# Gated cross-attention block: the last batches' low parts on VectorE, a relu block moved ahead of the gates, and two swaps in the first steps

## What is computed

```python
emb = ln(x) + ctx
q, k, v = emb @ wq + bq, emb @ wk + bk, emb @ wv + bv
ek, ew = exp(k - max_k), exp(pos_bias * band - max_w)      # band: |i - j| < 64
attn = (sigmoid(q) * (ew @ (ek * v)) / (ew @ ek)) @ wo + bo
a = ln(attn + emb) * gamma + beta
ff = relu(a @ w1 + b1) @ w2 + b2                            # 256 -> 1024 -> 256
x1 = x + tanh(g_xattn) * (ln(ff + a) * gamma + beta)
n = ln(x1); prev = n shifted by one row (zeros first)
xr, xk = mu_r * n + (1 - mu_r) * prev, mu_k * n + (1 - mu_k) * prev
r = sigmoid(xr @ W_r.T); kk = relu(xk @ W_k.T) ** 2
out = x1 + tanh(g_ffn) * r * (kk @ W_v.T)
```

## Time and profile before

| | us |
|---|---|
| median of 3 runs | 482.67 |
| lowest, highest | 480.25, 482.8 |
| the profiled execution, whole | 481.42 |
| its span in the trace | 479.7 |
| PE busy in the span | 456.3 (95%) |
| PE weight loads busy | 414.6 (86%) |
| DVE, ACT, POOL busy | 392.5, 239.8, 265.8 |

### The profile page before, as it was taken

One profiled execution on the slowest core, in us unless ns is written; L12 is line 12 of the kernel. 1 busy time (PEld: TensorE's weight loads), 2 busy tenths in 40 slices (PEclk: granted clock), 3 DMA queues, 4 the chain that ended last, 5 costly groups with the idle time before them and its releaser, 6 DMA issues.

```text
span 479.7 us, 8228 instructions
## 1 busy us (share of the span) xinstructions
PE 456.3 (95%) x3080; PEld 414.6 (86%) x3080; DVE 392.5 (82%) x729; ACT 239.8 (50%) x372; POOL 265.8 (55%) x243
## 2 busy tenths in 40 slices
PE   8989989899999999999999999999999998999966
PEld 8879789789889998989889998989889996978865
DVE  4998869997959987798959988698939975788886
ACT  3681662664373634755374644655263634546242
POOL 2574852663497256853497346952495237553552
PEclk9999999999999999999999999999999999999979
DMA  8741310110002200112002200111001100020002
GB/s 267 262 131 43 113 45 2 44 56 35 0 1 89 88 2 1 44 55 79 0 1 90 87 3 1 44 45 45 0 2 42 47 2 0 1 70 20 1 0 88
DMA packets 21896, 23.35 MB, mean 49 GB/s; under 512 B 993, under 2 KB 20961, under 8 KB 21857
## 3 DMA queue, kind: packets, MB, share of 16 engines
q1 hardware_dynamic: 20768, 21.26, 13.4%
q10 hardware_dynamic: 1088, 1.57, 1.0%
HBM read 18.64 MB, written 4.19 MB: 48 GB/s over the span
## 4 chain that ended last, share of the span: by engine, by line
PE 51%; issue 16%; POOL 14%; DVE 14%; ACT 4%; DMA 1%; POOLq 0%; DVEq 0%; ACTq 0%
PE ps L1344 46%; DVE y L673 5%; POOL hid_lo L225 3%; POOL xk_lo L225 3%; PE ps L1350 2%; DVE xk L741 2%; POOL a_rows L428 2%; PE ps L1359 1%; DVE y L670 1%; POOL x_beta L428 1%; POOL emb L428 1%; DMA x_in<-in_x 1%; ACT xk_hi L1127 1%; POOL rs_head L421 1%; ACT x_in L1055 1%
## 5 line engine op out<-in xcount | busy, mean ns | idle before, releaser
L1344 PE MATMUL ps<-w_hi,hid_hi 128*128 128x256 f32 x296 | 74.6, 289 | 2.4 <-DVE y L680 1.7
L1344 PE MATMUL ps<-w_lo,hid_hi 128*128 128x256 f32 x296 | 72.9, 282 | 0.0
L817 DVE SCALAR_TENSOR_TENSOR hid_lo<-ps,neg_b,hid 128x512 fp32r<-128x512 f32 x60 | 41.2, 737 | 34.0 <-ACT hid L1175 34.0
L1344 PEld LDWEIGHTS ps<-w_hi,hid_hi 128*128 128x128 f32 x296 | 56.2, 190 | 5.4 <-DVE y L680 4.2
L1344 PEld LDWEIGHTS ps<-w_lo,hid_hi 128*128 128x128 f32 x296 | 56.1, 190 | 0.0
L673 DVE RECIPROCAL y<-y 128x512 f32<-128x512 f32 x16 | 53.6, 3353 | 0.6
L1344 PE MATMUL ps<-a_hi,w_hi 128*128 128x512 f32 x128 | 50.9, 397 | 1.0 <-ACT a_hi L1157 0.8
L1344 PE MATMUL ps<-a_hi,w_lo 128*128 128x512 f32 x128 | 50.7, 396 | 0.0
L1169 ACT ACTIVATE hid_hi<-ps,b 128x512 fp32r<-128x512 f32 x60 | 37.9, 685 | 23.0 <-PE ps L1344 23.0
L225 POOL TENSOR_TENSOR ev_lo<-res,ev_hi 128x1024 fp32r<-128x1024 f32 x8 | 19.1, 2385 | 50.1 <-ACT ev_hi L1115 50.1
L1344 PE MATMUL ps<-w_hi,hid_lo 128*128 128x256 f32 x296 | 42.8, 285 | 2.5 <-POOL hid_lo L225 1.2
(11 more groups left out here) (251 smaller groups left out, 1329.4 us busy)
## 6 DMA issues: line engine op xcount, KB each, us to landing
x_in<-in_x SPq DMA_DIRECT2D x8, 512.0 KB, 4.1
emb<-in_ctx SPq DMA_DIRECT2D x8, 512.0 KB, 3.5
x_beta<-in_x SPq DMA_DIRECT2D x8, 512.0 KB, 3.7
out<-out_sb SPq DMA_DIRECT2D x7, 512.0 KB, 2.9
hid<-in_w SPq DMA_DIRECT2D x2, 512.0 KB, 6.9
x<-in_pos ACTq DMA_DIRECT2D x1, 512.0 KB, 4.6
out_sb<-in_pos ACTq DMA_DIRECT2D x1, 512.0 KB, 6.2
x<-in_w SPq DMA_DIRECT2D x1, 512.0 KB, 4.0
```

Source lines behind the costliest of these rows:

```text
L817: dve.scalar_tensor_tensor(out=tile(lo, b, T), in0=bank(relu_pair(n, q), b), scalar=neg_b1[:, m:m + 1], in1=tile(shifted, b, T), op0=ALU.m ...
L1344: return pe.matmul(o, s, m, start=start, stop=stop, skip_group_check=True)
```

## The change

- **Tail, DVE and POOL.** `sq_low(6)`, both `last_xr_low` and the square of batch 7's first half go from POOL to DVE. POOL keeps the low part of the first half's square. `xr_low(6)` on POOL now also waits for `x1_done`, which `last_finish(0)` gives.
- **Tail, orders.** DVE: `mix_r(6)` ahead of `last_sum(0)`, `last_finish(1)` ahead of `square(6)`, `last_normalise(1)` ahead of `last_mix_k(0)`, and the new instructions in between. ACT: `relu_k(6)` ahead of `last_normalise(0)`, `last_normalise(1)` ahead of `last_xk_high(0)`, and the last tanhs and squares in another order. PE: `turn_fin(6)` behind the first of the eight `add_last`.
- **Step 7.** `hidden(6, 2)` goes ahead of `ffn_r(5)` and writes pair 1; `hidden(6, 3)` writes pair 0. `ffn_v(5)`, which follows it into pair 0, waits for 28 blocks read instead of 27. The high and low part of `xr` of batch 5 go to `ew_hi`, `ew_lo`. The turning of batch 7 goes ahead of `add_hidden(6, 3)`.
- **Start and step 1.** PE: `hidden(0, 1)` ahead of the rest of `values(1)`. DVE: `hidden_low(0, 0)` ahead of `keep_values(1)`. ACT in step 1: the normalisation of batch 3's input behind `hidden_high(0, 3)`.

```diff
         def xr_split(n):
-            return (ew_hi, ew_lo) if isinstance(n, int) and n == BATCH - 2 else (xr_hi, xr_lo)
+            return (ew_hi, ew_lo) if isinstance(n, int) and n in (BATCH - 3, BATCH - 2) else (xr_hi, xr_lo)
...
         def relu_pair(n, q):
-            return (0, 2, 1, 0)[q] if is_last(n) else (0, 2, 0, 1)[q]
+            if is_last(n):
+                return (0, 2, 1, 0)[q]
+            return (0, 2, 1, 0)[q] if isinstance(n, int) and n == BATCH - 2 else (0, 2, 0, 1)[q]
...
             last_stats("ff", 0)
+            pool.wait_ge(x1_done, TT * b + 2)
             xr_low(pool, a)
...
             last_stats("fin", 1)
-            sq_low(pool, a)
-            last_xr_low(0)
-            pool.wait_ge(relu_k_done, BATCH)
-            pool.tensor_tensor(half(last_xk_t, 0), half(last_xk_t, 0), half(last_xk_t, 0), ALU.mult).then_inc(sq_done, 1)
-            last_xr_low(1)
             pool.wait_ge(sq_hi_done, BATCH)
...
+            hidden_low(0, 0)
             keep_values(1, 3)
-            hidden_low(0, 0)
...
+            mix_r(a)
             last_sum(0)
             last_ff_stats(0)
             last_scale(0)
-            mix_r(a)
...
             last_normalise(0)
+            last_finish(1)
             square(a)
-            last_finish(1)
             last_fin_stats(1)
             last_difference(0)
+            last_normalise(1)
             last_mix_k(0)
-            last_normalise(1)
+            sq_low(dve, a)
             last_xk_low(0)
             last_mix_r(0)
             last_difference(1)
             last_mix_k(1)
+            last_xr_low(0)
+            last_xk_low(1)
             last_mix_r(1)
-            last_xk_low(1)
+            last_square(0)
+            last_xr_low(1)
             gate_ffn(a)
-            dve.wait_ge(relu_k_done, BATCH + 1)
-            dve.tensor_tensor(half(last_xk_t, 1), half(last_xk_t, 1), bank(1, 1), ALU.mult).then_inc(last_sq, 1)
+            last_square(1)
             make_out(a)
...
-                if has(e):
+                if has(e) and i > 1:
                     normalise("head", e, x_in)
                 hidden_high(b, 3)
+                if i == 1:
+                    normalise("head", e, x_in)
...
-                relus_read(most(NQ * (n + 1) + 3, NQ * BATCH))
+                relus_read(NQ * (n + 2) if n >= BATCH - 3 else NQ * (n + 1) + 3)
                 rows_out(0, unit(7, 0), sq_hi, sq_lo, sq_lo_done, n + 1, fv_done, before_low=before_low)
...
                 hidden(0, 0, 0)
+                hidden(0, 1)
 
             values(1, 3, first_hidden)
-            hidden(0, 1)
...
+                if is_last(i):
+                    pe.wait_ge(den_read, DC * BATCH)
+                    hidden(b, 2)
                 if has(a):
                     ffn_r(a)
                     pe.wait_ge(sq_done, a + 1)
-                pe.wait_ge(emb_lo_done, most(b + 3, BATCH))
-                hidden(b, 2)
+                if not is_last(i):
+                    pe.wait_ge(emb_lo_done, b + 3)
+                    hidden(b, 2)
...
                 add_hidden(b, 2)
-                add_hidden(b, 3)
+                if not is_last(i):
+                    add_hidden(b, 3)
                 pe.wait_ge(norm_done["mid"], TT * (i + 1))
                 turn(2, norm, mid_turned)
+                if is_last(i):
+                    add_hidden(b, 3)
...
-            turn_fin(a)
             pe.wait_ge(ff_sum_done, DC * b)
             for h in range(2):
                 for q in range(NQ):
                     add_last(q, h)
+                    if h == 0 and q == 0:
+                        turn_fin(a)
```

More of the change, by code:

```diff
@@ L200, in flamingo_gated_block @@
         gated_done, out_done = sem("gated_done"), sem("out_done")
-        last_norm_dve, last_sq, last_sq_lo = sem("last_norm_dve"), sem("last_sq"), sem("last_sq_lo")
+        last_norm_dve, last_sq_lo = sem("last_norm_dve"), sem("last_sq_lo")
         def after(eng, s, count):
@@ L545, in last_stats @@
                                        ).then_inc(nmr_done["fin"], 1)
[L547 to L550, removed]
             a, b = BATCH - 2, BATCH - 1
@@ L1002, in last_xk_low, with last_xr_low, last_square @@
                                   ).then_inc(xk_lo_done, 1)
+            def last_xr_low(h):
+                dve.wait_ge(xr_hi_done, BATCH + h)
+                dve.tensor_tensor(half(xr_lo, h), half(last_xr_t, h), f32(half(xr_hi, h)), ALU.subtract
+                                  ).then_inc(xr_lo_done, 1)
+            def last_square(h):
+                dve.wait_ge(relu_k_done, BATCH + h)
+                dve.tensor_tensor(half(last_xk_t, h), half(last_xk_t, h), bank(1, h), ALU.mult).then_inc(sq_done, 1)
             def last_gate(h):
@@ L1130, in mixed_r_high @@
                 act.wait_ge(xr_done, DC * (n + 1))
-                if isinstance(n, int) and n == BATCH - 2:
+                if isinstance(n, int) and n in (BATCH - 3, BATCH - 2):
                     act.wait_ge(num_done, DC * BATCH)
+                    act.wait_ge(fr_done, BATCH - 3 if n == BATCH - 3 else BATCH - 2)
                 act.activation(xr_split(n)[0], xr, ACT.Copy).then_inc(xr_hi_done, 1)
@@ L1308, in last_square_high @@
                 act.wait_ge(fv_done, b)
-                act.wait_ge(*((sq_done, BATCH) if h == 0 else (last_sq, 1)))
+                act.wait_ge(sq_done, BATCH + h)
                 act.activation(half(sq_hi, h), half(last_xk_t, h), ACT.Copy).then_inc(sq_hi_done, 1)
@@ L1321, in _ @@
             mixed_r_high(a)
+            relu_k(a)
             last_normalise(0)
-            relu_k(a)
             square_high(a)
@@ L1332, in _ @@
             last_xk_high(1)
-            last_square_high(0)
             last_tanh_r(0)
             last_xr_high(1)
+            last_square_high(0)
             last_relu_k(1)
+            last_tanh_r(1)
             last_square_high(1)
-            last_tanh_r(1)
         @block.tensor
```

## The result

The changed kernel takes 484.1 us (median of 15 runs, 480.41 to 485.58), the kernel before in the same session 480.94 (15 runs, 479.97 to 482.8). The ratio is **1.006, with a 95% interval of 1.0042 to 1.0079**: slower by 0.6%. That is just over the 0.5% that the chances took as the line, and the interval holds the line too. The prediction was 485.0, and its range of 479.5 to 488.0 holds the time. The profiled execution of the changed kernel took 485.58 us, the slowest of the 15, with a span of 483.9. All profiles show one execution each.

The account below looks back on a forecast made before the run. PE, busy 95% of the span, was taken as the bound, so only its stops count. Start 0, step 7 +3.5 and tail -3.4 gave 482.8 against the median 482.67; 2.2 of clock made 485.0, range 479.5 to 488.0.

Parts of the forecast that it names:

- the chances: Odds on the whole change: slower 0.40, same 0.43, faster 0.17; 0.5% (2.4 us) counts as change, lines 480.3 and 485.1.
- Step 7, the wait that comes: PE waits 3.6 us at `ffn_v(5)` and 1.8 at the low part of `hidden(7, 0)`; everything 3.5 us later (2.7 to 4.0).
- The clock in step 7: Behind the new 3.6 us stop PE's granted clock falls to half, costing 2.2 us (0 to 3.0).
- The rival in which it stays up: In step 7 PE is dense around the stop, so the clock holds: 482.8 us, a wash; chance 0.24.
- the sum without clock: Whole kernel: 0 + 3.5 - 3.4 = +0.1 us, giving 482.8 against the median 482.67.
- The tail: New orders and work moved from POOL to DVE gain 3.4 us at the end (bounds 2.5 and 4.6).
- the old end, 477.12: End of the last DVE row before the change, 476.37 + 0.75, from which the tail's 3.4 us gain was counted.
- the new end, 473.7 in the sum: Tail's end on DVE: from 458.35, 15.6 us of work, less 0.7 overlap, plus 0.5 of waits on ACT.
- Start and step 1: 0 us: DVE's `hidden_low(0, 3)` still sets PE's pace; at most 0.7 gained, nothing lost.
- a second fall of the clock: Part of the more-lost rival: in step 1 (stops merged to 2.1 us) or the tail; another 2.0, 487.0; chance 0.18.
- the port at `beta_t`: Start, alternative cause in the more-lost rival: DVE waits out POOL's 2.41 us instruction, PE 1.7 us later; chance 0.18.
- The faster rival: Tail gains 4.6, start 0.7, step 7 costs only 2.7 with the clock up: 480.1 us; chance 0.18.

## Why the prediction was right, and where it wasn't

**Direction and size.** The step 7 edits cost more than the tail's gain, with the clock as the difference: this is what the runs show. Median to median it is +3.2 us (484.1 - 480.94), where the prediction had +2.3. The absolute time is off by as much the other way (484.1 for 485.0), since the kernel before was 1.7 faster in 15 runs than in the three it was predicted against. With the right base the same sum would have given 483.3. That the absolute time comes out within 0.9 us is in part this luck. The chances gave 0.40 to slower and 0.43 to no change, so the outcome wasn't the one they favoured.

**Step 7, the wait that comes.** Predicted 3.6 us ahead of `ffn_v(5)` and 1.8 ahead of the low part of `hidden(7, 0)`; measured 3.57 and 1.69. The total of 3.5 is 3.66 with the clock held up. The stop of 1.16 ahead of the output product, behind `ffn_r(5)`, is there, as its times imply (405.2 to 406.5). The chain relu, shifted relu, `hidden_low` was read off and moved unchanged.

**The clock in step 7.** Predicted 2.2 with bounds of 0 and 3.0; measured 2.66 in the profiles and 2.0 by the ratios. The rival in which it stays up (482.8) falls. Its argument, that PE is dense on both sides of the stop, doesn't hold here. The quickest of the 15 runs of the changed kernel, 480.41, was the one whose granted clock averaged 1.0 (0.984 to 0.993 in the others), so one execution in fifteen still escaped. It lies 0.1 to 0.4 us above the quick executions of before (479.97 to 480.33), and the sum without clock had +0.1.

**The tail.** Predicted -3.4 (bounds 2.5 and 4.6). The edits alone are 3.3 by the ratio, 3.5 by the medians and 4.6 between the profiled executions. That the typical gain is met is luck: two terms of the sum failed and cancelled. The first is the old end, 477.12. It is of an execution with the clock low for 6.9 us, and a shorter fall gives a stretch 1.1 to 1.2 us shorter; the working never took that out as a term, though the upper bound named it. The second is the new end, 473.7 in the sum and 472.4 in the run. `last_turn(1)` was to come 3.1 us early and came 3.9 early, because the last statistics ended at 455.55 instead of 455.9 and POOL took 1.5 us from there to its last nmr, where the sum had 1.95, about what it was before (1.92). And DVE's stretch behind that took 14.9 us instead of 15.4, so `last_turn(1)` comes 13.9 us before the last DVE row, not 15. `last_normalise(1)` was put at 0.43 and took 0.41. `mix_r(6)` does hold the port against `xk_low(6)`. In the changed kernel, DVE and POOL:

```profile
450.63 1.40 DVE L734 SCALAR_TENSOR_TENSOR xr<-out_sb,vec,xn_t 128x512 f32<-128x512 f32 x2
...
451.45 2.84 POOL L225 TENSOR_TENSOR xk_lo<-xk,xk_hi 128x1024 fp32r<-128x1024 f32 x1 [7.06 <-ACT xk_hi L1132]
```

POOL's takes 2.84 instead of 2.40, and costs nothing at the end: `last_finish(0)` still comes 0.5 us earlier than before (446.68 for 447.14 in the tail's edits alone).

**Start and step 1.** Predicted 0, measured 1.0013 (1.0 to 1.0026), about 0.6 us. PE's row is the same, behind `hidden_low(0, 3)`. The sum put the merged stop at nothing ("nothing lost"), while the rivals had it, 2.1 long, as a cause of a second fall of the clock. It is 2.15 long, and the fall is in all three profiles that have it and in one of nine that don't. That is strong evidence that part of the cost is there, short of a proof: no run fills this stop. The other part of that rival, the port at `beta_t`, did not happen: DVE took 0.35 us for it, as before:

```profile
62.43 0.35 DVE L868 TENSOR_SCALAR beta_t<-beta_t,gates 128x256 f32<-128x256 f32 x1
```

**The faster rival** wanted the tail's upper bound together with the clock up in step 7. Its tail came in the profile, its clock didn't.

## What to carry to other kernels

Before a block is moved ahead, look whose buffer it now writes: here a wait of 1.67 us was covered, and the next block that writes the same banks came to stand directly behind it and had to wait until they were read, for 3.57 us and a low clock. Price a stop on TensorE at its length plus what it may cost in clock, and where the stop can't be avoided, try filling it with products that nobody reads; here that paid about 2 us. Split a change that is a wash into its places: this one held a part worth -0.7%, and one that cost 1.1%. Before a difference between two profiles is put down to an edit, compare the granted clock of the stretch in both: the tail's 4.6 us held 1.1 us of it.

## What the hardware showed beyond that

- Twelve identity products (24 rows, 2.84 us) kept the granted clock at 1.00 through what was a stop of 3.57 us, with 0.89 us of it left. The two stops of the changed kernel's tail (1.77 and 0.69 us) left it at 1.00, the one of 3.57 us took it to 0.50 in all three profiles that have it.
- Shorter stops are not safe. With 0.72, 1.17 and 0.42 us in step 1, the clock fell in one profile of nine; with 2.15 and 0.42 there, in all three. In the old tail (1.53 and 2.98 us; 2.25 and 1.60 with the turn moved) it fell in all five profiles, for 3.4 to 6.9 us; in the new one (1.75 and 0.69) in none of six, nor with 1.74, 1.65 and 0.83. One profile can carry 1 to 2 us of this, so differences below that are settled by the timed runs.
- DVE's tile of 0.41 us took 2.33 when POOL had started 0.19 us earlier on SBUF, and POOL itself took 2.37. When DVE was first, POOL's instruction took 2.84 for 2.40. The Trainium skill ("SBUF — State Buffer", "SBUF: two separate sides") says that whichever of the two starts first, a GpSimd operation or a VectorE operation of the kinds it lists, holds the shared port pair for the whole instruction; these rows agree, in both directions.
